# A residual written into PSUM ahead of the bias products, in a fused macaron block (FFN, attention, FFN) on one Trainium2 core

## The reference

```
x = x + 0.5 * ffn(layernorm(x))
x = x + attn(layernorm(x))
x = x + 0.5 * ffn(layernorm(x))

ffn:  gates = softmax(x @ Wg + bg); take the two largest, scale them to sum to 1
      out = sum over the two experts e of gate_e * (x @ We[e] + be[e])     (8 experts, 256 -> 256)
attn: xp = x @ Wp.T + bp; q, k, v from xp; 16 heads of 16; each row attends to rows i-1, i, i+1
      out @ Wo.T + bo
```

## Time and profile before

| | |
|---|---|
| median of 3 runs | 1137.74 us |
| lowest, highest | 1134.66, 1139.28 us |
| the profiled execution, its own time | 1135.11 us |
| its span in the trace | 1133.3 us |
| mean granted TensorE clock | 0.976 |
| busy share PE / DVE / ACT / POOL | 94% / 84% / 46% / 63% |
| HBM traffic over the span | 18 GB/s |

### The profile page before, as it was taken

How to read it: one execution, slowest core, us unless ns; L and a number is a source line. 1 busy time by engine, 2 the same in 40 slices (tenths; PEclk the granted TensorE clock), 3 DMA queues, 4 the chain that set the end, 5 groups by cost and what they waited for, 6 DMA issues and landing times.

```text
span 1133.3 us, 17965 instructions
## 1 busy us (share of the span) xinstructions
PE 1070.8 (94%) x5459; PEld 889.8 (79%) x5459; DVE 950.8 (84%) x2675; ACT 518.8 (46%) x1181; POOL 714.8 (63%) x953
## 2 busy tenths in 40 slices
PE   4898799999999999999999999999999999998785
PEld 2676688888888888888888888888888888887563
DVE  3659789898898898888888989888889898988873
ACT  3253454444455544544555444445554444444331
POOL 2465466666676666666766676667666766563443
PEclk9899899999999999999999999999999999999988
DMA  5001000000000000000000000000000000000000
GB/s 162 10 30 35 12 15 6 19 20 20 19 19 20 14 6 19 20 19 20 20 19 11 10 19 20 19 20 19 20 12 8 19 20 20 10 10 10 10 10 19
DMA packets 12583, 23.05 MB, mean 20 GB/s; under 512 B 2212, under 2 KB 5812, under 8 KB 12488
## 3 DMA queue, kind: packets, MB, share of 16 engines
q1 hardware_dynamic: 9240, 13.37, 3.4%
q0 software_dynamic: 3248, 8.54, 2.7%
HBM read 12.47 MB, written 8.39 MB: 18 GB/s over the span
## 4 chain that ended last, share of the span: by engine, by line
PE 80%; DVE 9%; SPq 3%; DMA 2%; issue 2%; ACT 2%; POOL 1%; DVEq 0%; POOLq 0%; ACTq 0%
PE ffn_bank L889 18%; PE ffn_bank L891 18%; PE ffn_bank L890 18%; PE tr_bank L918 5%; PE tr_bank L930 4%; PE mix_bank L890 3%; PE mix_bank L891 3%; PE mix_bank L889 3%; SPq L243 2%; PE tr_bank L889 2%; DVE chain_sum L656 2%; PE mix_bank L955 1%; DMA we_raw<-in_L_ffn_We 1%; PE tr_bank L891 1%; PE tr_bank L890 1%
## 5 line engine op out<-in xcount | busy, mean ns | idle before, releaser
L889 PE MATMUL ffn_bank<-we_hi,T_hi 128*128 128x512 f32 x1024 | 416.3, 407 | 3.8 <-DVE chain_sum L656 2.5
L891 PE MATMUL ffn_bank<-we_hi,T_lo 128*128 128x512 f32 x1024 | 404.9, 395 | 0.0
L890 PE MATMUL ffn_bank<-we_lo,T_hi 128*128 128x512 f32 x1024 | 404.0, 395 | 0.0
L332 POOL TENSOR_TENSOR chain_sum<-chain_sum,we_raw 128x512 f32<-128x512 f32 x128 | 165.8, 1295 | 184.4 <-DVE chain_sum L656 184.4
L446 ACT ACTIVATE we_raw<-ffn_bank,gate 128x256 f32<-128x256 f32 x512 | 208.1, 479 | 134.7 <-PE ffn_bank L891 134.6
L889 PEld LDWEIGHTS ffn_bank<-we_hi,T_hi 128*128 128x128 f32 x1024 | 195.3, 191 | 46.1 <-issue 4.6
L891 PEld LDWEIGHTS ffn_bank<-we_hi,T_lo 128*128 128x128 f32 x1024 | 194.5, 190 | 43.2
L890 PEld LDWEIGHTS ffn_bank<-we_lo,T_hi 128*128 128x128 f32 x1024 | 195.6, 191 | 35.5
L409 ACT CAST T_hi<-tr_bank 128x512 fp32r<-128x512 f32 x128 | 75.0, 588 | 121.8 <-PE tr_bank L918 121.6
L656 DVE SCALAR_TENSOR_TENSOR chain_sum<-ffn_bank,gate,base 128x256 f32<-128x256 f32 x128 | 61.4, 479 | 77.2 <-POOL base L324 49.3
L656 DVE SCALAR_TENSOR_TENSOR chain_sum<-ffn_bank,gate,chain_sum 128x256 f32<-128x256 f32 x256 | 110.7, 473 | 8.4 <-PE ffn_bank L891 8.4
(11 more groups left out here) (128 smaller groups left out, 1862.2 us busy)
## 6 DMA issues: line engine op xcount, KB each, us to landing
out_x<-y SPq DMA_DIRECT2D x31, 256.0 KB, 2.0
we_raw<-in_L_ffn_We SPq DMA_DIRECT2D x2, 1024.0 KB, 13.9
x_in<-in_L_attn_x,x_row POOLq DMA_INDIRECT x60, 2.9
x_in<-in_L_attn_x SPq DMA_DIRECT2D x2, 256.0 KB, 7.5
moved_qk<-qk SPq DMA_DIRECT2D x4, 124.0 KB
w_raw<-in_L_attn_Wq SPq DMA_DIRECT2D x1, 256.0 KB, 2.8
w_raw<-in_L_attn_Wk SPq DMA_DIRECT2D x1, 256.0 KB, 3.0
w_raw<-in_L_attn_Wv SPq DMA_DIRECT2D x1, 256.0 KB, 3.9
```

The lines of the kernel that those rows point to most:

```text
L332: nc.gpsimd.tensor_tensor(chain_sum[:, f, t], chain_sum[:, f, t], scaled[:, f, t, 1], ALU.add).then_inc(done, 1)
L889: nc.tensor.matmul(dest, hi[:, t, k, :], w_hi_[:, k, c0:c1], start=(first and k == 0), stop=False, skip_group_check=not first)
L890: nc.tensor.matmul(dest, hi[:, t, k, :], w_lo_[:, k, c0:c1], start=False, stop=False, skip_group_check=not first)
L891: last = nc.tensor.matmul(dest, lo[:, t, k, :], w_hi_[:, k, c0:c1], start=False, stop=(k == KB - 1), skip_group_check=not first)
```

## The change

The base is now put together in PSUM.

- ScalarE has a new `residual_step(f, n)`: it copies x_in (FFN1) or x2 (FFN2), 128x512, into `bias_bank[f]`. It stands behind the copy of v and ahead of the cast of `gateT`, FFN2's first. It waits for what read the bank last (v_copied or qk_copied, both ScalarE's own; `base_done`, its own too, at the ends of the pipeline) and for x.
- PE's bias products no longer start an accumulation (`start=False` on both), so they add onto the residual. They wait for `residual_set` in place of the banks' last readers.
- ScalarE's copy out of the bank, which stood at the same place, writes `base` directly and is now called `base_step`. It waits for the last chain that read `base`.
- GpSimd's two additions per step (line 324), and the buffer `bias_sum`, are gone. The gather of x and VectorE's `x2_step` wait for `residual_set` instead of `base_done`.
- In the setup, the product for bo_all goes to a half of tr_bank 0 instead of mix_bank 0.

```diff
-                if (s - 4).within(GROUPS):
-                    base_step(FFN2, s - 4)
...
-                if (s + 1).within(PAIRS):
-                    base_step(FFN1, s + 1)
...
-                    await_(pool, base_done[FFN1], (s + 1).times(1, 1))
+                    pool.wait_ge(residual_set[FFN1], s.const + 2)
...
-            def bias_step(f, n):
+            def residual_step(f, n):
+
+                if f == FFN1:
+                    await_x(act, n)
+                    if n.const == 0:
+                        act.wait_ge(setup_dve, 6)
+                    elif n.const == 1:
+                        act.wait_ge(base_done[FFN1], 1)
+                    else:
+                        act.wait_ge(v_copied, n.const - 1)
+                else:
+                    act.wait_ge(x2_done, n.const + 1)
+                    if (n + 3).within(PAIRS):
+                        act.wait_ge(qk_copied, 2 * (n.const + 4))
+                    else:
+                        act.wait_ge(base_done[FFN2], n.const)
+                nc.scalar.copy(bias_bank[f][:, :], (x_in if f == FFN1 else x2)[:, n.slot].rearrange("p t n -> p (t n)")).then_inc(residual_set[f], 1)
+
+            def base_step(f, n):
                 act.wait_ge(bias_done[f], n.times(1, 1))
-                await_(act, base_done[f], n.times(1))
-                nc.scalar.copy(bias_sum[:, f].rearrange("p t n -> p (t n)"), bias_bank[f][:, :]).then_inc(bias_copied[f], 1)
+                await_(act, chain_done[f], n.times(8))
+                nc.scalar.copy(base[:, f].rearrange("p t n -> p (t n)"), bias_bank[f][:, :]).then_inc(base_done[f], 1)
...
+                if ffn2:
+                    residual_step(FFN2, s - 4)
+                if (s + 1).within(PAIRS):
+                    residual_step(FFN1, s + 1)
                 gateT_step(s + 1)
...
-                await_(dve, base_done[FFN2], (a - 1).times(1))
+                await_(dve, residual_set[FFN2], (a - 1).times(1))
...
-                if f == FFN1:
-                    await_(pe, v_copied, (s - 1).times(1, 1))
-                else:
-                    await_(pe, qk_copied, after_pair(s - 1, 2))
-                if s.reg is None:
-                    await_(pe, bias_copied[f], (s + 1 if f == FFN1 else s - 4).times(1))
+                pe.wait_ge(residual_set[f], s.const + 2 if f == FFN1 else s.const - 3)
                 for t in range(2):
                     last = nc.tensor.matmul(bias_bank[f][:, t * D:(t + 1) * D], gateT[:], be_rows[:, 2 * f + t, :],
-                                            start=(t == 0), stop=True, skip_group_check=(t == 1))
+                                            start=False, stop=True, skip_group_check=True)
```

More of the change, by code:

```diff
@@ L142, in build @@
         gateT = sb("gateT", [PART, PART], f32r)
-        bias_sum = sb("bias_sum", [PART, NF, 2, D])
         base = sb("base", [PART, NF, 2, D])
@@ L194, in build @@
         bias_done = [sem(f"bias_done{f}") for f in range(NF)]
-        bias_copied = [sem(f"bias_copied{f}") for f in range(NF)]
+        residual_set = [sem(f"residual_set{f}") for f in range(NF)]
         base_done = [sem(f"base_done{f}") for f in range(NF)]
@@ L314, in rstd_step @@
                 nc.gpsimd.tensor_tensor(shift[:, ln], minus_mean[:, ln], rstd[:, ln], ALU.mult).then_inc(done, 1)
-            def base_step(f, n):
-                if f == FFN1:
-                    await_x(pool, n)
-                else:
[L321 to L325, removed]
             def sum_step(f, n, t):
@@ L454, in seed_step @@
                     act.wait_ge(setup_dve, 7)
-                readers = [(bias_copied[FFN1], n.const + 2) if (n + 1).within(PAIRS) else (v_copied, n.const),
-                           (bias_copied[FFN2], n.const - 3) if (n - 4).within(GROUPS) else (qk_copied, 2 * n.const)]
+                readers = [(base_done[FFN1], n.const + 2) if (n + 1).within(PAIRS) else (v_copied, n.const),
+                           (base_done[FFN2], n.const - 3) if (n - 4).within(GROUPS) else (qk_copied, 2 * n.const)]
                 for t, (read, value) in enumerate(readers):
@@ L528, in body @@
                     v_step(s - 1)
+                if ffn2:
+                    residual_step(FFN2, s - 4)
+                if (s + 1).within(PAIRS):
+                    residual_step(FFN1, s + 1)
                 gateT_step(s + 1)
                 if ffn2:
-                    bias_step(FFN2, s - 4)
+                    base_step(FFN2, s - 4)
                 if (s + 1).within(PAIRS):
-                    bias_step(FFN1, s + 1)
+                    base_step(FFN1, s + 1)
                 if s.within(PAIRS):
@@ L783, in _ @@
             dve.wait_ge(small_loaded, 16 * 4)
-            nc.vector.tensor_tensor(bo_all[:], mix_bank[0][:, 0:D], bo_all[:], ALU.add).then_inc(setup_dve, 1)
+            nc.vector.tensor_tensor(bo_all[:], tr_bank[0][:, D:2 * D], bo_all[:], ALU.add).then_inc(setup_dve, 1)
             dve.wait_ge(setup_dve, 3)
@@ L1012, in _ @@
             for mb in range(KB):
-                last = nc.tensor.matmul(mix_bank[0][:, 0:D], bv_wide[:, mb, :], woT[:, mb, :],
+                last = nc.tensor.matmul(tr_bank[0][:, D:2 * D], bv_wide[:, mb, :], woT[:, mb, :],
                                         start=(mb == 0), stop=(mb == KB - 1))
```

## The result

Six runs of each kernel, side by side: before 1136.62 us median (1133.90 to 1139.49), after 1122.80 us (1121.02 to 1125.42). The ratio is 0.988, 95% interval 0.986 to 0.990: faster by 13.8 us, where the forecast was 6.75 us and a time between 1125.5 and 1137.5 us. The profiled execution of after has a span of 1120.4 us against 1133.3.

A forecast was written before the change was run, and what follows sets the result against it. PE was taken to bound the steady part, leaving the ends and few waits to win. Filling 0, steady -1.5, steps 31 to 33 -1.5, -1.05, -1.0, clock -1.7: -6.75 us, from 1137.74 to 1131.0 us; range 1125.5 to 1137.5.

The forecast's parts named there:

- PE bounds the steady part, with its matmuls back to back: From 180 to 1020 us PE is busy 838.7 of 840 us, so gains lie in the ends and few waits.
- steady part, -1.5, bounds 0 and -2.2: Steady steps: PE's weight loads no longer wait for T_lo, 2.2 us in 12 waits; -1.5 us.
- The copies at nothing: ScalarE's two added copies per steady step, 1.18 us, fit its 1.24 us idle time, 0.93 us more free; cost 0.
- The filling steps at 0: First steps, where PE waits for qk copies: the base is not on that path; gain 0, bounds +-0.5 us.
- Step 31, -1.5: Draining step: attention products lose 1.11 us beside GpSimd's base addition, plus some 0.4 us from the base wait; -1.5 us.
- The next two terms, -1.05 and -1.0: Draining steps 32 and 33: attention products no longer meet the base addition, so PE's chain_sum waits shrink; -1.05 and -1.0 us.
- The clock, -1.7: Drain: with PE's 2.95 us wait shortened to about 1.45, TensorE's clock fall behind it goes; -1.7 us, bounds 0 and -1.7.
- x_bo takes the base's place: Rival: GpSimd's x_bo moves earlier and meets the steady attention products; 0.26 us lost a step, 1144.7 us; chance 0.08.
- the cover at bank 1: Steady step: the chain freeing bank 1 ends early enough to leave 0.84 us before PE needs it.
- products of 3 us in the steady steps: Sign of being wrong: VectorE's attention products, forecast at 1.86 and 2.06 us in steps 31 to 33, take 3 us in steady steps.
- The step length of 32.3 us: Expected sign in the changed kernel's profile: the steady step still takes 32.3 us; a longer one would refute the prediction.

The follow-up runs named there:

- e1: Changed kernel with only FFN1's base in PSUM; FFN2's addition given back to GpSimd: 1124.92 us, ratio 0.988 to 0.991.
- e4: Kernel before, nothing through PSUM, with GpSimd's FFN1 base addition moved between FFN2's two sum steps: 1126.09 us, ratio 0.990 to 0.994.
- e9: Changed kernel with two more unread ScalarE copies ahead of gateT's cast in each step that has FFN2: 1133.51 us, ratio 0.994 to 0.997.
- e0: The changed kernel run once more, unaltered, as yardstick: 1122.87 us, ratio 0.986 to 0.991 to the kernel before.
- e11: Changed kernel with ScalarE's seeds of Q and K moved to the end of its step: 1120.52 us, ratio 0.983 to 0.986.
- e7: Changed kernel with GpSimd's x_bo behind FFN2's first sum and the seeds of Q and K at the end of ScalarE's step: 1111.09 us.
- e12: Kernel before, nothing through PSUM: FFN1's base between FFN2's sums, x_bo behind the first, Q and K seeds at ScalarE's step end: 1123.85 us.
- e2: Changed kernel with only FFN2's base in PSUM; FFN1's addition given back to GpSimd at its old place: 1146.68 us, ratio 1.007 to 1.011.
- e8: Kernel with only FFN2's base in PSUM, with GpSimd's x_bo moved behind FFN2's first sum: 1133.45 us, ratio 0.993 to 0.997.
- e10: Changed kernel with an unused 1.74 us VectorE reduction where the wait for FFN1's base was: 1144.47 us, ratio 1.004 to 1.007.
- e3: Kernel before with GpSimd's FFN1 base addition moved ahead of both of FFN2's sum steps: 1137.84 us, ratio 0.999 to 1.001.
- e5: Changed kernel with two GpSimd additions of 128x512, result unread, at the two old places: 1126.14 us, ratio 0.989 to 0.994.
- e6: Changed kernel with GpSimd's x_bo (x1 plus output bias) moved behind FFN2's first sum: 1121.82 us, ratio 0.985 to 0.989.

## Why the prediction was wrong

The sign was right, the size half, and the time lies outside the range. By its steps:

- **"PE bounds the steady part, with its matmuls back to back": failed, and with it the size.** This came from the busy share of 838.7 in 840 us. PE lost 0.34 us in every step in stalls of about 0.1 us. The term "steady part, -1.5, bounds 0 and -2.2" was taken from the list of waits, which notes T_lo in 12 of 26 steps with 2.2 us. It measured -8.6 (before against after), and -8.2 to -8.9 by the steps of e1 and e4. That the wait for the base was behind these stalls was right; what it cost was not. By the spans this term is 7.1 us beyond its forecast, the filling steps add 1.3, and the drain gave 2.98 for 5.25: together the 6.1 us between 6.75 and 12.8.
- **The copies at nothing: right**, with 0.85 us of cover left (e9).
- **The filling steps at 0: not to be told from the scatter**. Before and after differ by 1.3 us at transpose 5, which is outside the bounds of 0.5, but before and e0 by 0.55, and e1 comes there 1.3 us later than before.
- **Step 31, -1.5: the mechanism failed.** The products fell to 2.07 us as forecast, but then the chain waited:

```profile
1016.89 0.48 DVE L662 SCALAR_TENSOR_TENSOR chain_sum<-ffn_bank,gate,base 128x256 f32<-128x256 f32 x1 [1.45 <-PE ffn_bank L897]
```
```profile
1014.85 1.09 ACT L461 COPY mix_bank<-bqkv 128x512 f32<-128x512 f32 x2
1015.88 1.56 ACT L448 ACTIVATE we_raw<-ffn_bank,gate 128x256 f32<-128x256 f32 x4
```

  The list names PE, but what came last is ScalarE's scaling, behind the seeds. PE's wait stayed at 2.92 us here, and at 2.92 to 2.97 in every kernel with early seeds; it fell to 2.49 with late seeds (e11) and to 1.90 with x_bo late too (e7; 2.51 in e12, which has both late but keeps FFN2's addition). The prediction had not asked what is late next. The step itself, from transpose 31 to 32, took 28.1 us in before, 29.2 in after and 28.0 in e0: nothing was won there.
- **The step ahead of it, 30, was left out.** From transpose 30 to 31 before takes 31.47 us and after 30.60. The attention products meet the base addition there too, which the prediction missed when it counted three such places; there are four:

```profile
993.33 2.96 DVE L678 TENSOR_TENSOR prod<-qk 128x512 f32<-128x512 f32 x3
```

  The 0.87 us are not the encounter's but FFN1's base wait once more: 31.46 us in e2 and e8, which keep the wait and have the products at 1.87, and 30.6 in e1 and e4, which lose the wait and keep the products at 2.96. e10, with 1.74 us of work in place of the wait, takes 30.89.
- **The next two terms, -1.05 and -1.0: the first right, the second right by half, as PE's waits have it.** PE's wait fell by 1.05 and by 0.43 us. The steps became 1.3 and 1.85 us shorter between before and after (1.3 and 1.1 to e0); in the second one the mean clock differs too, 0.86 in before, 0.99 in after and 0.95 in e0. The steps that hold them took 22.9 to 23.8 and 23.2 to 23.9 us in the five kernels with FFN2's addition on GpSimd (before, e1, e3, e4, e12), and 21.7 to 21.9 and 22.1 to 23.7 in the ten without (e5 left out). That is 1.4 us and 0.7 in the mean.
- **The clock, -1.7: failed.** The wait did not shrink, and behind its 2.92 us the clock fell in after too, for longer. The link to the length of that wait does not hold: in e9 the wait is 2.94 us and the clock stays up in the step that holds it, 26.44 us for 29.21 in after, while in e7 the wait is 1.90 us and the mean clock of the step 0.94 as in before.

```profile
1025.79:1052.23 26.44, 23.50 (x127) 19.86 (x126) 20.24 (x60) 13.08 (x29) 9.95 (x15) 1.00 0.03 11
```

  That step takes 27.0 to 28.6 us in most kernels and 26.0 to 26.5, at a clock of 1.00, in e5, e9 and e11. So what the fall costs was sized about right (e5 and e9 are 1.6 us below e0, with the same wait), and what decides whether it comes I can't say from single executions.
- **The rival "x_bo takes the base's place": right in its mechanism**, down to the 1.1 us and to the condition ("if VectorE starts no earlier than now"). Its price was too low: 0.26 us a step by the cover at bank 1, where e2 shows 0.54 by way of the exponential. In the changed kernel the lead pays for it. The lock that the Trainium skill describes ("SBUF — State Buffer", section "Who interferes with whom") agrees with the 2.97 us rows; whether it costs depends on the path it falls on, as e6 shows, where it goes and nothing is won.

Shown by runs: that FFN1's wait was the steady loss (gone in e1 and e4, kept in e8 with a step of 32.37 us, and put back as work in e10), that load alone is not (e5), that FFN2's half alone loses by x_bo (e2, e8), and that two paths bind behind (e6, e7, e11). Argued only: that FFN2's addition acts in the last steps through the products alone, and that the 0.27 us between e12 and e7 are FFN2's half. One of the prediction's own signs of being wrong came true, products of 3 us in the steady steps, and the kernel was faster all the same: VectorE's lead, which the prediction had named against that rival, paid for them. The step length of 32.3 us, which it expected to stay, became 32.05.

## What to carry to other kernels

A busy share of 100% and a short list of waits don't prove that TensorE sets the pace. Compare the spacing of its instructions within a step with the best spacing of the same form, and look for a producer that ends just as it starts; 0.1 us at four places of 25 steps was 8.6 us here. Before an idle time of another engine is called harmless, ask for each of its results how long before its use it is ready. And a piece of work that is taken away moves its neighbours into new company: before coding the removal, try moving the one step that others wait for, since that gave most of this gain (e4; e12, with two more moves, nearly all), and at a place only slightly different gave none (e3).

## What the runs showed of the hardware

- A VectorE instruction that meets GpSimd's 128x512 addition pays for the rest of the addition, however small it is itself: the copy of 128x2 takes 0.17 us alone and 1.27 beside it, the maximum of 128x32 0.18 and up to 0.75. By the Trainium skill ("SBUF — State Buffer", section "Who interferes with whom") copies too can take the shared port pair; the trace agrees with 1.27 us.
- The second maximum takes 1.28 us in all 25 steady steps of before and after, beside GpSimd's chain_sum addition. It stands on the way to the exponential. Moving that addition was not tried.
- A delay that PE's row gives as a wait of 0.16 us cost 0.40 us (e9), and in before 13 to 14 of 25 steps lost their 0.34 us with no wait for T_lo listed at all.
- ScalarE's copy into PSUM takes what the copy out of it takes, 0.59 us for 128x512, and the bias products that add onto it take 0.28 us each, as before.
